# P times V of two pairs in a row, in every second attention step

## The chip, the cores and the metric

The kernel runs on one core of a Trainium2 chip. The metric is the device time of the kernel in microseconds (us), the median of several runs. The engines of the core work side by side and meet through semaphores: TensorE (PE, matmuls; PEld its weight loads), VectorE (DVE), ScalarE (ACT), GpSimd (POOL) and SyncE (SP), which here issues transfers.

## The reference, cut to what matters

The input x is 16 items of 512 tokens x 256. Each item goes through a half feed-forward block, an attention block and another half feed-forward block:

```
x = x + 0.5 * ffn(layernorm(x));  x = x + attn(layernorm(x));  x = x + 0.5 * ffn(layernorm(x))
attn: qkv = x @ w_qkv; 16 heads of 64; sim = (q*SCALE) @ k.T - slope_h*|i-j|, causal
      out = softmax(sim) @ v; return out @ w_out + b_out
ffn:  gelu(x @ w1 + b1) @ w2 + b2      (256 -> 1024 -> 256)
```

## The kernel before, in words

Everything is in float32; a matmul of weights with activations is done as three matmuls (high with high, high with low, low with high). Each engine has its own instruction stream, written out by hand in the order in which it is to run; there is no planner. An engine takes its instructions strictly in that order, and a wait holds all that stands behind it.

The outer loop runs over the items b = 0 to 15. Within an item the heads are taken as eight pairs c = 0 to 7 (two heads a pair). One step c of the attention loop (TensorE: `attention`, L489; ScalarE L650; VectorE L874; GpSimd L1023) has these parts:

- `scores(b, c)` (L432): TensorE computes Q times K transposed of the pair, 8 blocks, in PSUM banks 0 to 5. It waits for the copy of the pair's Q by ScalarE (`proj_copy`), and for VectorE to have read the blocks before.
- `biased` (L833, VectorE): adds the distance bias, finds the row maxima and writes P to SBUF. Blocks go in the order i = 3, 2, 0, 1 (`QORDER`).
- `exps` (L638, ScalarE): exponentials in place, with their sums. `inverse` (L827, VectorE) inverts the sums, `normalise` (L1018, GpSimd) multiplies by them.
- `turned` (L845, VectorE): transposes P in place in 32 x 32 blocks, in two halves. In step c VectorE does `biased(b, c, 3)`, `inverse(b, c-1, 0)`, both halves of `turned(b, c-1)`, and then `biased` of the other blocks. (In step 7 of all items but the last `turned(b, 6, 1)` stands ahead of `biased(b, 7, 3)`.)
- `spread` (L241): 16 transfers bring the blocks of P to the other partitions, into PT (two buffers, by c mod 2). SyncE issues 11 of them, GpSimd 5. They wait for `turned(b, c, 0)` and for P times V of pair c-2, which read the same buffer of PT. P has three buffers.
- `values(b, c)` (L445): TensorE computes P times V of the pair, 12 matmuls in one bank. It waits for the spread of the pair, and for V. `out_copy` (L646, ScalarE) copies its output to SBUF.
- `proj_tile` (L413): K and Q of pair c+1 and one tile of V (none in step 7, two in step 6) by TensorE; ScalarE copies them. They and `values` take turns in banks 6 and 7 (`bank_for`, L341: the bank after `turn[0]` of those in `among[0]`, once what it holds has been read).

Before the change TensorE's step c is scores(c), K and Q of pair c+1, a V tile, values(c-2). In steps 6 and 7 the work of the next item stands between (two layer norm transposes, three of its up projections). ScalarE's step is out_copy(c-3), exps(c,3), copies of K and Q, exps(c,2), copy of V, exps(c,0), exps(c,1).

Of the kernel before, what the change touches and what calls it, by code (L numbers as in the profile page):

```python
def build(nc, x_d, w_qkv_d, w_out_d, b_out_d, w1_d, b1_d, w2_d, b2_d, y_d):
# [11 lines left out]
    NT, NK, NM, NC = T // 128, D // 128, F // 128, H // 2  # L13
# [97 lines left out]
    def v_tiles(c):  # L111
        return {6: [("v", 3, 0), ("v", 3, 1)], 7: []}.get(c, [("v", c // 2, c % 2)] if c >= 2 else [])
# [8 lines left out]
    def steps_v(b, c):  # L121

        if b == 0 and c <= 3:
            return v_tiles(2) + v_tiles(3) if c == 1 else []
        return v_tiles(c)
# [127 lines left out]
    with block:  # L253
# [50 lines left out]
        def _(e):  # L304
            def mm(out, lhsT, rhs, first, last):
                return e.matmul(out, lhsT, rhs, start=first, stop=last)  # L306
# [31 lines left out]
            turn = [7]  # L338
# [93 lines left out]
            def scores(b, c):  # L432
                e.wait_ge(s_pc.sem, s_pc.at((b, ("q", c))))
                for i in QORDER:
                    w = 128 * (i + 1)
                    for h in range(2):
                        if i != 0:
                            bank_free(h + {3: 0, 2: 2, 1: 4}[i])
                            held[h + {3: 0, 2: 2, 1: 4}[i]] = ("scores", b, c, 0 if i == 2 else i, h)
                        hs = slice(64 * h, 64 * h + 64)  # L440
                        keys = qk[c % 2][hs, 1, 0:w].rearrange("p (j m s) -> p m j s", m=4, s=32)
                        mm(score_block(h, i), qk[c % 2][hs, 0, i * 128:i * 128 + 128], keys,
                           True, True).then_inc(s_qk.sem, 1)

            def values(b, c):  # L445
                pv = bank_for(("values", b, c))
                e.wait_ge(s_pc.sem, s_pc.at((b, ("v", c // 2, 1))))
                if b == NB - 1 and c in LAST:
                    e.wait_ge(s_ls[c].sem, s_ls[c].at((b, c)))
                    e.wait_ge(s_la[c].sem, s_la[c].at((b, c)))  # L450
                else:
                    e.wait_ge(s_pt[c % 3].sem, s_pt[c % 3].at((b, c)))
                e.wait_ge(s_pp[c % 3].sem, s_pp[c % 3].at((b, c)))
                for n, (j, blocks) in enumerate(RUNS):
                    i = blocks[0]
                    for h in range(2):
                        p = PT[c % 2][:, 0, block_at(h, i) + 32 * j]
                        step = block_at(h, blocks[-1]) - block_at(h, i)
                        turned = AP(p.tensor, p.offset, [[4 * GW, 128], [step, len(blocks)], [GW, 4], [1, 32]])
                        last = mm(pv[64 * h:64 * h + 64, 128 * i:128 * i + 128 * len(blocks)],  # L460
                                  v[(c // 2) % 2][:, j, 2 * (c % 2) + h, :], turned, n == 0, n == len(RUNS) - 1)
                last.then_inc(s_pv.sem, 1)
# [26 lines left out]
            def attention(b):  # L489
                more = b + 1 < NB  # L490
                begin(b)
                for c in range(2, NC):
                    scores(b, c)
                    if c + 1 < NC:
                        proj_tile(b, ("k", c + 1))
                        proj_tile(b, ("q", c + 1))
                    for tile in steps_v(b, c):
                        proj_tile(b, tile)
                    if more and c == NC - 1:
                        up(1, b + 1, range(2))  # L500
                        among[0] = (0, 1)
                        up(1, b + 1, [2])
                    if more and c == NC - 2:
                        ln_transpose(1, b + 1, 0)
                        among[0] = (5,)
                        ln_transpose(1, b + 1, 1)
                        among[0] = (6, 7)
                    values(b, c - 2)
                    if more and c == NC - 2:
                        turn[0] = 5  # L510
                if more:
                    among[0] = (2, 3, 4, 5)
                    up(1, b + 1, range(3, 6))
                    values(b, NC - 2)
                    among[0] = range(8)
                    up(1, b + 1, range(6, NM))
                    for t in range(3):
                        dn(1, b + 1, t)
                    values(b, NC - 1)
                    dn(1, b + 1, 3)  # L520
                else:
                    among[0] = range(4)
                    for c in range(4):
                        out_part(c, range(NT))
                    among[0] = range(4, 8)
                    values(b, NC - 2)
                    for c in range(4, 6):
                        out_part(c, range(NT))
                    values(b, NC - 1)
                    out_part(6, range(NT))  # L530
                    out_part(7, range(NT))
# [44 lines left out]
        def _(e):  # L576
# [61 lines left out]
            def exps(b, c, i):  # L638
                for h in range(2):
                    e.wait_ge(s_tt.sem, s_tt.at((b, c, i, h)))  # L640
                    p = p_block(c, h, i)
                    r = 2 * (c % 2) + h
                    e.activation(p, p, ACT.Exp, bias=mx[:, r, i:i + 1], scale=-1.0,  # L643
                                 accum_out=sm[:, r, i:i + 1]).then_inc(s_ex.sem, 1)

            def out_copy(b, c):  # L646
                e.wait_ge(s_pv.sem, s_pv.at((b, c)))
                e.activation(o[:, c, :], bank_of(("values", b, c)), ACT.Copy).then_inc(s_oa.sem, 1)

            def attention(b):  # L650
                more = b + 1 < NB
                if b == 0:
                    exps(b, 0, 3)
                    proj_copy(b, tiles[3])
                proj_copy(b, ("k", 1))
                proj_copy(b, ("q", 1))
                for i in QORDER[0 if b > 0 else 1:]:
                    exps(b, 0, i)
                exps(b, 1, 3)
                proj_copy(b, ("k", 2))  # L660
                if b == 0:
                    proj_copy(b, ("q", 2))
                exps(b, 1, 2)
                for tile in steps_v(b, 1)[:1]:
                    proj_copy(b, tile)
                exps(b, 1, 0)
                if b > 0:
                    proj_copy(b, ("q", 2))
                for tile in steps_v(b, 1)[1:]:
                    proj_copy(b, tile)  # L670
                exps(b, 1, 1)
                for c in range(2, NC):
                    if c >= 3:
                        out_copy(b, c - 3)
                    exps(b, c, 3)
                    if c + 1 < NC:
                        proj_copy(b, ("k", c + 1))
                        proj_copy(b, ("q", c + 1))
                    exps(b, c, 2)
                    for tile in steps_v(b, c)[:1]:  # L680
                        proj_copy(b, tile)
                    exps(b, c, 0)
                    for tile in steps_v(b, c)[1:]:
                        proj_copy(b, tile)
                    exps(b, c, 1)
                    if more and c == NC - 2:
                        ln_hi(1, b + 1, 0)
                        ln_hi(1, b + 1, 1)
                if more:
                    gelu(1, b + 1, range(2))  # L690
                    out_copy(b, NC - 3)
                    gelu(1, b + 1, range(2, 6))
                    out_copy(b, NC - 2)
                    gelu(1, b + 1, range(6, NM))
                    out_hi_first(b)
                    out_copy(b, NC - 1)
                else:
                    for c in range(2):
                        out_part_hi(c)
                    spread(e, b, NC - 2, LAST_ACT, s_la[NC - 2])  # L700
                    for c in range(2, 5):
                        out_part_hi(c)
                    out_copy(b, NC - 3)
                    out_part_hi(NC - 3)
                    spread(e, b, NC - 1, LAST_ACT, s_la[NC - 1])
                    for c in (NC - 2, NC - 1):
                        out_copy(b, c)
                        out_part_hi(c)
# [386 lines left out]
```

## Time and profile before

| | before |
|---|---|
| median of 3 runs, us | 2165.0 (2164.84 to 2168.31) |
| span of the profiled execution, us | 2165.1 |
| TensorE busy, us | 2126.9 (98%) |
| VectorE / ScalarE / GpSimd busy, us | 1501.1 / 1238.3 / 1056.3 |
| mean granted TensorE clock | 0.996 |
| transfers of P into PT: by SyncE, by GpSimd | 1398, 640 |

The span runs from the first to the last instruction of one profiled execution; no other time of that execution is given, and the span equals the median of the runs within 0.1 us.
### The profile page before, as it was taken

How to read it: one execution, taken by the hardware profiler on the slowest of the kernel's cores; microseconds unless marked ns; L12 is line 12 of the kernel's file. 1: busy time of each engine (PE TensorE's matmuls, PEld its weight loads, DVE VectorE, ACT ScalarE, POOL GpSimd, SP SyncE). 2: the span in 40 equal slices, each digit the busy share in tenths (PEclk: the TensorE clock that was granted, in tenths of full speed). 3: DMA queues.
4: the chain of work that ended last, by engine and by line, in shares of the span. 5: the costliest groups of instructions: out<-in, count | busy, mean ns of one | idle time of the engine just before them, and what ended most of it. 6: DMA issues, size and time to landing. Idle time of an engine off the chain costs nothing.

```text
span 2165.1 us, 41855 instructions
## 1 busy us (share of the span) xinstructions
PE 2126.9 (98%) x14720; PEld 1739.2 (80%) x14720; DVE 1501.1 (69%) x4031; ACT 1238.3 (57%) x3111; POOL 1056.3 (49%) x1772
## 2 busy tenths in 40 slices
PE   7999999999999999999999999999999999999997
PEld 6688787887878788787887978878787787877866
DVE  6866767667676676776768676676766767667674
ACT  5745646466464664736557365574646646466472
POOL 2744627446273553725537174472744627355371
PEclk9999999999999999999999999999999999999999
DMA  3422505234061441514315052250523405134051
GB/s 132 132 74 75 141 1 158 57 89 127 11 157 50 107 108 31 155 30 118 98 46 145 25 140 76 71 144 3 157 59 93 123 12 155 50 106 110 26 140 51
DMA packets 109985, 193.91 MB, mean 90 GB/s; under 512 B 34512, under 2 KB 53200, under 8 KB 109776
## 3 DMA queue, kind: packets, MB, share of 16 engines
q1 hardware_dynamic: 88816, 137.95, 22.8%
q0 software_dynamic: 20480, 52.47, 9.8%
q8 instruction: 117, 1.92, 0.4%
q10 hardware_dynamic: 480, 0.82, 0.1%
q14 instruction: 92, 0.75, 0.1%
HBM read 14.95 MB, written 8.39 MB: 11 GB/s over the span
## 4 chain that ended last, share of the span: by engine, by line
PE 89%; SPq 4%; DVE 3%; DMA 2%; issue 1%; ACT 1%; POOL 1%; DVEq 0%; POOLq 0%
PE ps L306 87%; SPq L249 3%; PE ps L360 2%; DVE P L848 1%; DMA PT<-P 1%; ACT P L643 1%; DMA out_y<-x 0%; POOL P L1021 0%; POOL PT L249 0%; DVE P L840 0%; DMA raw<-in_L_ffn_w 0%; DVE gl L754 0%; DVE xtl L754 0%; DVE x L787 0%; ACT v L594 0%
## 5 line engine op out<-in xcount | busy, mean ns | idle before, releaser
L1021 POOL TENSOR_SCALAR P<-P,rs 128x512 f32<-128x512 f32 (+3 forms) x1024 | 539.1, 545 | 423.0 <-DVE rs L831 419.7
L643 ACT ACTIVATE P<-P,mx 128x512 f32<-128x512 f32 (+3 forms) x1024 | 562.7, 552 | 186.2 <-DVE mx L840 186.1
L249 POOL DMA_DIRECT2D PT<-P x640 | 322.2, 509 | 249.5 <-DVE P L848 235.6
L848 DVE STREAM_TRANSPOSE P<-P 128x1792 f32<-128x1792 f32 (+1 forms) x256 | 372.3, 1483 | 7.3 <-POOL P L1021 6.8
L306 PE MATMUL ps<-PT,v 128*64 128x256 f32 (+1 forms) x3072 | 305.2, 348 | 8.9 <-DMA PT<-P 8.5
L306 PE MATMUL ps<-qk 64*128 64x512 f32 (+3 forms) x2048 | 311.0, 443 | 0.7 <-ACT qk L594 0.7
L306 PE MATMUL ps<-w2h,gh 128*128 128x256 f32 x1024 | 292.6, 286 | 0.3 <-DVE gl L754 0.3
L306 PE MATMUL ps<-w2l,gh 128*128 128x256 f32 x1024 | 289.7, 283 | 0.0
L306 PE MATMUL ps<-w2h,gl 128*128 128x256 f32 x1024 | 289.6, 283 | 0.0
L306 PEld LDWEIGHTS ps<-PT,v 128*64 128x64 f32 x3072 | 205.5, 137 | 103.8 <-issue 15.1
L594 ACT ACTIVATE qk<-ps 128x512 f32<-128x512 f32 x256 | 153.0, 598 | 230.5 <-PE ps L306 230.5
L840 DVE CUSTOM_DVE_ANT_1 P<-ps,dist 128x384 f32<-128x384 f32 (+2 forms) x768 | 272.3, 414 | 0.0
L612 ACT ACTIVATE gt<-ps,b1c 128x512 f32<-128x512 f32 x256 | 172.9, 688 | 163.3 <-PE ps L306 129.8
L306 PEld LDWEIGHTS ps<-qk 64*128 64x128 f32 x2048 | 166.2, 187 | 114.9 <-issue 73.3
L787 DVE TENSOR_TENSOR x<-ps,x 128x256 f32<-128x256 f32 x192 | 81.0, 422 | 255.5 <-PE ps L306 255.4
L840 DVE CUSTOM_DVE_ANT_0 P<-ps,dist 128x512 f32<-128x512 f32 x256 | 165.7, 684 | 124.9 <-PE ps L306 124.9
L1009 POOL TENSOR_TENSOR rstd<-ve,mhalf 128x4 f32<-128x4 f32 (+1 forms) x50 | 65.2, 1305 | 356.3 <-DVE ve L771 356.3
L306 PE MATMUL ps<-xth,wqh 128*128 128x512 f32 x512 | 210.2, 411 | 1.5 <-DVE xtl L754 1.5
L306 PEld LDWEIGHTS ps<-w2h,gh 128*128 128x128 f32 x1024 | 196.1, 192 | 9.9 <-issue 7.5
L306 PE MATMUL ps<-xtl,wqh 128*128 128x512 f32 x512 | 201.4, 393 | 0.0
L306 PE MATMUL ps<-xth,wql 128*128 128x512 f32 x512 | 200.3, 391 | 0.0
L306 PEld LDWEIGHTS ps<-w2l,gh 128*128 128x128 f32 x1024 | 196.1, 192 | 1.8
(85 smaller groups left out, 4394.7 us busy)
## 6 DMA issues: line engine op xcount, KB each, us to landing
PT<-P SPq DMA_DIRECT2D x1398, 80.0 KB, 2.6
PT<-P POOLq DMA_DIRECT2D x640, 80.0 KB, 2.7
x<-in_L_attn_x SPq DMA_DIRECT2D x16, 512.0 KB, 4.9
out_y<-x SPq DMA_DIRECT2D x15, 512.0 KB, 3.2
raw<-in_L_ffn_w SPq DMA_DIRECT2D x2, 512.0 KB, 5.8
raw<-in_L_ffn_w SPq DMA_DIRECT2D x1, 1024.0 KB, 8.7
rawq<-in_L_attn_w_qkv SPq DMA_DIRECT2D x1, 1024.0 KB, 6.8
rawk<-in_L_attn_w_qkv SPq DMA_DIRECT2D x1, 1024.0 KB, 8.8
```

The source lines that it names most:

```text
L249: e.dma_start(PT[c % 2][32 * m:32 * m + 32, g, :], P[c % 3][32 * g:32 * g + 32, m, :]).then_inc(landed.sem, 16)
L306: return e.matmul(out, lhsT, rhs, start=first, stop=last)
L360: last = e.transpose(dst[:, col:col + 128], xn[:, t, k * 128:(k + 1) * 128], ident[:, :])
L594: e.activation(dst, src, ACT.Copy).then_inc(s_pc.sem, 1)
L612: e.activation(gt[m % 3][:, :], bank_of(("up", f, b, m)), ACT.Gelu, bias=b1c[:, m:m + 1]).then_inc(s_gl.sem, 1)
L643: e.activation(p, p, ACT.Exp, bias=mx[:, r, i:i + 1], scale=-1.0, accum_out=sm[:, r, i:i + 1]).then_inc(s_ex.sem, 1)
L787: e.tensor_tensor(xb[b % 2][:, t, :], bank_of(use)[:, 0:D], xb[b % 2][:, t, :], ALU.add).then_inc(events.sem, 1)
L840: e.tensor_tensor_reduce(out=p_block(c, h, i), in0=score_block(h, i).rearrange("p (m n) -> p m n", m=4), in1=dist[:, :, 128 - 32 * (i + 1) ...
L848: e.transpose(p, p).then_inc(s_tr.sem, 1)
L1009: e.tensor_tensor(rstd[:, L - 1, ts], ve[:, L - 1, ts], mhalf[:, ts], ALU.pow).then_inc(s_pw.sem, 1)
L1021: e.tensor_scalar(p, p, rs[:, 2 * (c % 2) + h, i:i + 1], 1.0, ALU.mult, ALU.mult).then_inc(s_nz.sem, 1)
```

## The change

In the steps c = 3, 5 and 7 TensorE does P times V of pairs c-3 and c-2 directly behind the scores of pair c, ahead of the projections; in the even steps it does none. ScalarE's order follows: in an odd step out_copy(c-3) comes behind exps(c,3) and out_copy(c-2) behind exps(c,2), and the copies of K, Q and V come behind exps(c,0) and exps(c,1). In the even steps its order is as before, without an output copy. The output copy of pair 5 leaves the row of GELUs behind the loop. The banks' turn is set at the start of step 7. VectorE's, GpSimd's and SyncE's streams are not changed.

```diff
--- before.py
+++ after.py
@@ -491,6 +491,11 @@
                 begin(b)
                 for c in range(2, NC):
                     scores(b, c)
+                    if c % 2:
+                        if c == NC - 1:
+                            turn[0] = 5
+                        values(b, c - 3)
+                        values(b, c - 2)
                     if c + 1 < NC:
                         proj_tile(b, ("k", c + 1))
                         proj_tile(b, ("q", c + 1))
@@ -505,9 +510,6 @@
                         among[0] = (5,)
                         ln_transpose(1, b + 1, 1)
                         among[0] = (6, 7)
-                    values(b, c - 2)
-                    if more and c == NC - 2:
-                        turn[0] = 5
                 if more:
                     among[0] = (2, 3, 4, 5)
                     up(1, b + 1, range(3, 6))
@@ -670,26 +672,34 @@
                     proj_copy(b, tile)
                 exps(b, 1, 1)
                 for c in range(2, NC):
-                    if c >= 3:
+                    exps(b, c, 3)
+                    if c % 2:
                         out_copy(b, c - 3)
-                    exps(b, c, 3)
-                    if c + 1 < NC:
+                        exps(b, c, 2)
+                        out_copy(b, c - 2)
+                        exps(b, c, 0)
+                        if c + 1 < NC:
+                            proj_copy(b, ("k", c + 1))
+                        exps(b, c, 1)
+                        if c + 1 < NC:
+                            proj_copy(b, ("q", c + 1))
+                        for tile in steps_v(b, c):
+                            proj_copy(b, tile)
+                    else:
                         proj_copy(b, ("k", c + 1))
                         proj_copy(b, ("q", c + 1))
-                    exps(b, c, 2)
-                    for tile in steps_v(b, c)[:1]:
-                        proj_copy(b, tile)
-                    exps(b, c, 0)
-                    for tile in steps_v(b, c)[1:]:
-                        proj_copy(b, tile)
-                    exps(b, c, 1)
+                        exps(b, c, 2)
+                        for tile in steps_v(b, c)[:1]:
+                            proj_copy(b, tile)
+                        exps(b, c, 0)
+                        for tile in steps_v(b, c)[1:]:
+                            proj_copy(b, tile)
+                        exps(b, c, 1)
                     if more and c == NC - 2:
                         ln_hi(1, b + 1, 0)
                         ln_hi(1, b + 1, 1)
                 if more:
-                    gelu(1, b + 1, range(2))
-                    out_copy(b, NC - 3)
-                    gelu(1, b + 1, range(2, 6))
+                    gelu(1, b + 1, range(6))
                     out_copy(b, NC - 2)
                     gelu(1, b + 1, range(6, NM))
                     out_hi_first(b)
@@ -700,7 +710,6 @@
                     spread(e, b, NC - 2, LAST_ACT, s_la[NC - 2])
                     for c in range(2, 5):
                         out_part_hi(c)
-                    out_copy(b, NC - 3)
                     out_part_hi(NC - 3)
                     spread(e, b, NC - 1, LAST_ACT, s_la[NC - 1])
                     for c in (NC - 2, NC - 1):
```

## Rows read from the trace of the kernel before

**Rows 1.** The profile's page: busy time, share of the span, instructions.

```profile
PE 2126.9 (98%) x14720; PEld 1739.2 (80%) x14720; DVE 1501.1 (69%) x4031; ACT 1238.3 (57%) x3111; POOL 1056.3 (49%) x1772
```

**Rows 2.** TensorE's waits: us in total, times, longest.

```profile
PE ps L306 <- DMA PT<-P: 8.5, 11, 2.0
```

**Rows 3.** Timeline, TensorE, fifth item: start us, us, engine, line, operation, what, count.

```profile
596.93 0.70 PE L306 MATMUL ps<-qk 64*128 64x512 f32 x2
...
603.34 0.28 PE L306 MATMUL ps<-wql,xth 128*128 128x256 f32 x1
603.46 0.28 PE L306 MATMUL ps<-wqh,xtl 128*128 128x256 f32 x1
603.67 2.38 PE L306 MATMUL ps<-PT,v 128*64 128x256 f32 x24
605.98 0.70 PE L306 MATMUL ps<-qk 64*128 64x512 f32 x2
...
608.34 0.50 PE L306 MATMUL ps<-xth,wqh 128*128 128x512 f32 x1
608.68 0.40 PE L306 MATMUL ps<-xtl,wqh 128*128 128x512 f32 x1
...
612.72 0.44 PE L306 MATMUL ps<-PT,v 128*64 128x256 f32 x2
...
615.03 0.70 PE L306 MATMUL ps<-qk 64*128 64x512 f32 x2
```

**Rows 4.** Timeline, VectorE, the same step (2.61 is idle time before).

```profile
607.14 0.69 DVE L840 CUSTOM_DVE_ANT_0 P<-ps,dist 128x512 f32<-128x512 f32 x1 [2.61 <-PE ps L306]
...
608.46 2.87 DVE L848 STREAM_TRANSPOSE P<-P 128x1792 f32<-128x1792 f32 x2
```

**Rows 5.** Timeline, SyncE's queue, last issues of pairs 1 and 3.

```profile
610.07 0.59 SPq L249 DMA_DIRECT2D PT<-P  x1
...
628.09 0.59 SPq L249 DMA_DIRECT2D PT<-P  x1
```

**Rows 6.** Chain that ended last, fourth item, around pair 2's P times V.

```profile
487.32 2.05 DMA PT<-P
...
489.62 9.12 PE ps L306 x64
```

**Rows 7.** Timeline, TensorE and SyncE, second and sixth item: scores, last issue.

```profile
199.36 0.70 PE L306 MATMUL ps<-qk 64*128 64x512 f32 x2
...
211.65 0.59 SPq L249 DMA_DIRECT2D PT<-P  x1
...
747.71 0.70 PE L306 MATMUL ps<-qk 64*128 64x512 f32 x2
...
759.67 0.69 SPq L249 DMA_DIRECT2D PT<-P  x1
```

**Rows 8.** Timeline, TensorE and SyncE, fifth item, steps 6 and 7.

```profile
633.12 0.70 PE L306 MATMUL ps<-qk 64*128 64x512 f32 x2
...
644.49 0.70 PE L306 MATMUL ps<-qk 64*128 64x512 f32 x2
...
646.15 0.59 SPq L249 DMA_DIRECT2D PT<-P  x1
...
657.83 0.44 PE L306 MATMUL ps<-PT,v 128*64 128x256 f32 x2
```

**Rows 9.** Timeline, ScalarE, fifth item, copy of Q in step 3.

```profile
611.39 0.60 ACT L594 ACTIVATE qk<-ps 128x512 f32<-128x512 f32 x1 [0.76 <-PE ps L306]
```

**Rows 10.** Timeline, TensorE, after idle time (in brackets, with its releaser).

```profile
73.88 1.48 PE L306 MATMUL ps<-PT,v 128*64 128x256 f32 x11 [2.05 <-DMA PT<-P]
...
2114.45 0.53 PE L306 MATMUL ps<-woh,fh 128*128 128x256 f32 x1 [2.49 <-DVE fl L754]
...
2117.77 0.36 PE L306 MATMUL ps<-woh,fh 128*128 128x256 f32 x1
```

**Rows 11.** Stretch: us, busy us of five engines, PEclk, DMA share, GB/s.

```profile
2116.00:2118.00 2.00, 2.00 (x12) 2.00 (x11) 0.20 (x1) 0.00 (x0) 0.90 (x2) 0.51 0.84 264
```

## The prediction

> **What bounds the kernel now.** I read the busy table, then TensorE's own waits, then the timeline of one item (the fifth, b = 4) engine by engine. In the busy table TensorE is at 98% [rows 1], and the table of its waits holds only 8.5 us of waiting for the spread transfers, in 11 places, none over 2.0 us [rows 2]. So it is a kernel in which time is TensorE's stream of work, and the question for any change of order is whether that stream still finds its data ready. One step of the steady part is 9.05 us: scores at 605.98, K, Q and V projections from 608.34, P times V at 612.72, next scores at 615.03 [rows 3].
>
> I write S(c) for the start of a step's scores, PV(c) for the start of P times V of pair c. From the rows: scores take 2.36 us (605.98 to 608.34), PV 2.31 (603.67 to 605.98), the three projections 4.38 (608.34 to 612.72) [rows 3].
>
> What PV(c-2) waits for is a long chain that starts at S(c-1). VectorE writes the first biased block 1.16 us after those scores (607.14), then inverts, and turns pair c-2 in place, ending at 608.46 + 2.87 = 611.33, S + 5.35 [rows 4]. Only then can SyncE issue its 11 spread transfers, one behind the other: for pair 1 the last issue is at 610.07 [rows 5], which is S(2) + 13.14 [rows 3]. Where TensorE did wait, the last issue at 487.32 landed after 2.05 us and PV began at 489.62 [rows 6]: a PV can start 2.30 us after the last issue. In the fifth item pair 1 is therefore ready at 610.07 + 2.30 = 612.37, and TensorE came to it at 612.72 [rows 3]. The slack is 0.35 us. This is what the 98% hides: the PV stands about as early as its data allow.
>
> **The change, part by part.**
>
> *TensorE, odd steps.* PV(c-2) is moved ahead of K, Q and V, and PV(c-3) from the end of the even step before to a place just behind S(c). The even step becomes scores and three projections: 2.36 + 4.38 = 6.74 us. This uses that scores enter behind a projection as PV does; PV entered 0.21 us behind the last V matmul (603.46 to 603.67) [rows 3], which I take for both. In the odd step TensorE wants PV(c-3) at S(c) + 2.36 and PV(c-2) at S(c) + 4.67, that is at S(c-1) + 6.74 + 4.67 = S(c-1) + 11.41. Before, the same PV(1) came at S(2) + 15.79. It is asked for 4.4 us earlier, and the chain that makes its data is not touched: S(c-1), VectorE's order, and SyncE's 11 issues stay.
>
> *The first such place, c = 3.* Ready at S(2) + 13.14 + 2.30 = +15.44, wanted at +11.41: a stall of 4.03 us. TensorE then has 2.31 of PV and 4.38 of projections to S(4), at S(2) + 22.13, against 615.03 - 596.93 = 18.10 before: 4.03 us lost. In the second item, where the last issue is earliest, it is S(2) + 12.29 (199.36 to 211.65) [rows 7], a loss of 3.2; worked as here, the mean over the 16 items is 3.9 us.
>
> *The second, c = 5.* Pair 3's last issue is at 628.09, S(4) + 13.06 [rows 3, 5]; in the sixth item it is only S(4) + 11.96 (747.71 to 759.67) [rows 7], since one slow issue is missing. Losses 3.97 and 2.8; the mean over the items is 3.4.
>
> *The third, c = 7.* Step 6 is longer (a second V tile, eight transposes). From S(6) at 633.12 to PV(6) at 657.83 it was 24.71 us [rows 8]. Step 6 alone was 11.36 (to S(7) at 644.49). The order now is step 6 without PV (11.36 - 2.31 = 9.05), scores, PV(4), PV(5), six up tiles, PV(6). PV(5) is wanted at S(6) + 13.72 and is ready at 646.15 + 2.30 = +15.33 [rows 8]: 1.6 us of stall, of which about 1.4 is lost up to PV(6); where pair 5's issues end a microsecond earlier I put the loss at 0.4. I take 0.8 between them. In the last item PV(5) waited already, and I count nothing.
>
> *Even steps, PV(c-3), and the batch's other PVs.* PV(c-3) was ready a step earlier: nothing. PT has two buffers, so the spread of pair c-1 now waits for PV(c-3) in odd steps, on SyncE and on GpSimd's queue. That PV ends at S(c) + 4.67, the turn at S(c) + 5.35: nothing, and the work queued behind that wait is not held. In a stalled step SyncE itself is issuing pair c-2 until about S(c) + 7, so pair c-1 starts 1.5 us late; it is wanted a whole pair of steps later, so this costs nothing.
>
> *ScalarE.* out_copy(c-2) now stands amid the exponentials, waits for PV(c-2), and behind it are exps(c,0), the K copy, exps(c,1) and the Q copy, on which S(c+1) waits. With P = PV(c-2): copy of the output P + 2.4 to 3.0, exps 0.8, K copy (ready at about P + 4.0) to P + 4.6, exps 1.0, Q copy to P + 6.2. TensorE wants S(c+1) at P + 6.69. Covered, by 0.5 us only. In the even step the order is as before and the Q copy ends at S + 6.01 (611.99) [rows 9], TensorE wants the next scores at S + 6.74: covered by 0.7 us.
>
> *Switches of tile shape.* Scores, PV and projections use the array in three shapes. The first projection matmul behind scores takes 0.34 us to the next where 0.23 is usual (608.34 to 608.68) [rows 3]; with about 0.1 ahead of it, a switch is some 0.2 us. Two steps had six of them and now have five, since PV follows PV; the new one, scores to PV, no row shows: its bounds are 0 and 0.4, and I take the nearest rows' 0.2. So 48 places gain 0.1 us on average between the bounds: 5 us. The Trainium skill (TensorEngine Tiling (Array Packing), Key Properties) says that a change of tiling mode drains TensorE; the rows agree with 0.2 us. By that rule alone, with all data in time, the change would give 48 x 0.2 = 10 us, which is the rival on the other side.
>
> *TensorE's clock.* After an idle 2.05 us (at 73.88) the granted clock stayed at 2.4 GHz; after an idle 2.49 us (at 2114.45) [rows 10] it was at 1.2 GHz (0.51 in the stretch 2116 to 2118) [rows 11] and the 256-column matmuls came every 0.221 us from 2114.45 to 2117.77 (15 intervals), where they come every 0.12 at the full clock (603.34 to 603.46) [rows 3, 10]. Such a stretch costs 15 x 0.10 = 1.5 us. My stalls at c = 3 and 5 are 2.9 to 4.4 us, 32 of them, all longer than 2.49. Bounds are 0 and 32 x 1.5 x 2 = 96 us (two stretches each). One row at 2.49 us doesn't say that every idle of that kind does it, so I let three in four do it: 36 us. The Trainium skill (TensorE: Matmul & The Clock Gate, HAM oscillation) tells of this pattern: a wait for data that comes back in each round throws the engine back to the low clock each time. By that rule it would be all 32, 48 us and 2338 us in total; without it the sum ends at 2290.
>
> **Sum.** 16 x (3.9 + 3.4 + 0.8) = 130; less 5; plus 36: 161 us. The profiled span is 2165.1 us, the median of the three runs 2165.0, so nothing of size lies around the span. 2165 + 161 = 2326 us.
>
> **Rivals.**
> 1. *Stalls, but the clock holds.* 2165 + 130 - 5 = 2290 us. For it: one fall at one idle of 2.49 us is thin, and PV and scores may keep the clock up. Against: the stalls here are longer. 0.23.
> 2. *ScalarE becomes the gate.* The 0.5 us of cover goes if the output copy or the exponentials come 1.5 us later than worked out; S(c+1) is then 1 us late in each odd step: 48 us more, 2372. 0.07.
> 3. *The other side: the data are in time.* It takes the last issue to be by S(c-1) + 11.41 - 2.30 = 9.11, nearly 3 us sooner than the earliest shown, 11.96 [rows 7]; only if VectorE turned pair c-2 before it needs S(c-1) could that be, and its first biased block stands ahead in its order [rows 4]. Then TensorE gains the switches alone, 48 x 0.2 = 10 us: 2155. 0.05.
> 4. *Half of it.* The spread of odd pairs is quicker in the new rhythm (fewer slow issues, 1 us less in each), or the loss is given back at an item's end: stalls of 2 us at c = 3 and 5, none at 7, no clock falls: about 2225 us. 0.08.
>
> **How the numbers follow.** My forecast has 0.57. Its own range is 2295 to 2360: stall means 0.5 us either way (16 each) and the clock at 15 to 50 us. Rival 1 is inside the range if it reaches down to 2265; rival 2 ends at about its top. 2265 to 2370 leaves out rivals 3 and 4 and half of 2, under 2 in 10. A measurement of this kernel can tell about 0.2% (4 us) from no change: faster 0.05 (rival 3), the same 0.02, slower 0.93.
>
> **What would show it.** Right: TensorE's waits for the spread transfers grow from 8.5 us to about 150, in about 45 places, at PV(1), PV(3), PV(5), with last issue to PV at 2.30 us; no wait at PV(0), (2), (4); busy share down to some 92%; S(2) to S(4) 22 us with the clock full, more with it low; the granted clock's mean near 0.98; no wait of TensorE for ScalarE at scores. Wrong: PV(c-2) starting 11.4 us behind S(c-1) without a wait; the waits in full but the clock at 1.00 (rival 1); S(c+1) released by a Q copy (rival 2).

## The result, and the profile after

| | before | after |
|---|---|---|
| median of 4 runs, us | 2164.92 (2164.64 to 2168.31) | 2336.22 (2327.07 to 2337.73) |
| ratio, 95% interval | | 1.0779 (1.0759 to 1.0800) |
| span of the profiled execution, us | 2165.1 | 2333.3 |
| mean granted TensorE clock | 0.996 | 0.974 |

The change costs 7.8%: 2336 us where 2326 was predicted, in a range of 2265 to 2370. The page's busy table has the same number of instructions on every engine, and nearly the same busy time on all but TensorE:

```profile
PE 2178.3 (93%) x14720; PEld 1777.4 (76%) x14720; DVE 1500.7 (64%) x4031; ACT 1244.4 (53%) x3111; POOL 1051.2 (45%) x1772
```

The profiled execution itself was timed at 2335.1 us, 1.8 us more than its span, and so it is in the other runs. TensorE's share fell from 98% [rows 1] to 93%, though its busy time grew by 51 us: the same 14720 matmuls, part of them at the low clock. Its waits (us in total, times, longest), which stood at 8.5 us in 11 places [rows 2]:

```profile
PE ps L306 <- DMA PT<-P: 119.5, 41, 5.1
...
PE ps L306 <- DVE xtl L763: 7.5, 17, 1.5
...
PE ps L306 <- ACT qk L596: 2.1, 3, 0.8
```

The wait for the spread transfers is now the one of size, and no wait for ScalarE is. The timeline of TensorE in the fifth item, steps 2 to 7 (the answer to [rows 3, 8]; in brackets the idle time and its releaser):

```profile
638.36 2.43 PE L306 MATMUL ps<-qk 64*128 64x512 f32 x16
...
645.10 2.43 PE L306 MATMUL ps<-qk 64*128 64x512 f32 x16
647.46 2.38 PE L306 MATMUL ps<-PT,v 128*64 128x256 f32 x24
653.48 4.53 PE L306 MATMUL ps<-PT,v 128*64 128x256 f32 x24 [3.64 <-DMA PT<-P]
...
662.70 2.43 PE L306 MATMUL ps<-qk 64*128 64x512 f32 x16
669.44 2.43 PE L306 MATMUL ps<-qk 64*128 64x512 f32 x16
671.79 2.38 PE L306 MATMUL ps<-PT,v 128*64 128x256 f32 x24
677.86 2.38 PE L306 MATMUL ps<-PT,v 128*64 128x256 f32 x24 [3.68 <-DMA PT<-P]
684.57 2.43 PE L306 MATMUL ps<-qk 64*128 64x512 f32 x16
693.63 2.42 PE L306 MATMUL ps<-qk 64*128 64x512 f32 x14
696.35 0.70 PE L306 MATMUL ps<-qk 64*128 64x256 f32 x2 [0.30 <-DVE xtl L763]
696.98 2.38 PE L306 MATMUL ps<-PT,v 128*64 128x256 f32 x24
699.72 2.38 PE L306 MATMUL ps<-PT,v 128*64 128x256 f32 x24 [0.36 <-DMA PT<-P]
```

Read it from start to start. The even step is 6.74 us (638.36 to 645.10), PV(0) starts 2.36 us behind the scores without a wait, and PV(1), asked for at S(2) + 11.41, starts at S(2) + 15.12: a stall of 3.71 us. It then takes 4.53 us where PV(0) took 2.38. From PV(1) to S(4) it is 9.22 us; from PV(3) to S(6) it is 6.71, which is the sum of a PV and three projections at the full clock.

The chain that ended last, in the same place (start us, us, what), shows what PV(1) stood behind:

```profile
641.04 2.80 DVE P L857 x2
...
650.41 0.59 SPq L249
...
651.04 2.19 DMA PT<-P
653.24 0.25 issue
653.48 10.39 PE ps L306 x52
```

The turn of pair 1 ends at 643.84, then come SyncE's 11 issues, then the landing of the last: the chain of [rows 5, 6] in the same order, with the engine now waiting at its end. From the start of the last issue to PV(1) it is 2.44 us here, where 2.30 was reckoned. For the granted clock, stretches of four us from the start of three PVs on (us, busy us of five engines, PEclk, DMA share, GB/s): PV(1) and PV(3) of the fifth item, and PV(3) of the third, with that PV's own row behind them:

```profile
653.48:657.48 4.00, 4.00 (x22) 2.70 (x24) 1.04 (x9) 0.70 (x4) 3.96 (x9) 0.50 0.78 208
```
```profile
391.57:395.57 4.00, 4.00 (x25) 3.01 (x26) 3.60 (x17) 1.66 (x5) 3.26 (x6) 0.62 0.52 141
...
677.86:681.86 4.00, 4.00 (x31) 3.22 (x32) 3.02 (x11) 1.98 (x8) 3.97 (x7) 1.00 0.77 211
```
```profile
391.57 3.61 PE L306 MATMUL ps<-PT,v 128*64 128x256 f32 x24 [2.69 <-DMA PT<-P]
```

0.50 is 1.2 GHz, 1.00 is 2.4 GHz. PV(1) of the fifth item ran at the low clock, PV(3) of the same item at the full one, behind a wait that was as long. In PV(3) of the third item the clock fell on the way: 0.62 is the mean of four us that began at the full clock and ended at the low one.

Where the 168 us are (16 items, each stretch from start to start, after less before): S(2) to S(4) **+90.4**, S(4) to S(6) **+62.6**, S(6) to PV(6) **+14.9**, all the rest +0.3. Of these, what PV(1) to S(4) and PV(3) to S(6) take beyond 6.69 us, the length at the full clock, goes with the low clock: 29.3 us in all 16 items at c = 3, 12.5 us in 7 of the 16 at c = 5. **Together: 42 us of clock, 126 us of waiting** (the little that the new order gives back is already taken off, see Switches below).

### The profile page after: what moved, and what is told of

The parts are those of the page before. It is cut to its first block, busy times and chain, and to the rows that moved or that the text cites. A ratio compares the mean times of both kernels' runs of the same rounds, so it can differ in the third digit from the quotient of the medians.

```text
span 2333.3 us, 41855 instructions
## 1 busy us (share of the span) xinstructions
PE 2178.3 (93%) x14720; PEld 1777.4 (76%) x14720; DVE 1500.7 (64%) x4031; ACT 1244.4 (53%) x3111; POOL 1051.2 (45%) x1772
## 4 chain that ended last, share of the span: by engine, by line
PE 68%; SPq 14%; DVE 7%; DMA 5%; issue 3%; ACT 2%; POOL 0%; ACTq 0%; DVEq 0%
PE ps L306 66%; SPq L249 14%; DVE P L857 4%; DMA PT<-P 4%; PE ps L360 1%; DMA out_y<-x 1%; ACT P L645 1%; DVE P L849 1%; DVE xtl L763 1%; ACT v L596 0%; DVE x L796 0%; ACT qk L596 0%; DMA raw<-in_L_ffn_w 0%; POOL P L1030 0%; ACT xth L606 0%
## 5 line engine op out<-in xcount | busy, mean ns | idle before, releaser
L1030 POOL TENSOR_SCALAR P<-P,rs 128x512 f32<-128x512 f32 (+3 forms) x1024 | 532.0, 537 | 569.7 <-DVE rs L840 566.3
L306 PE MATMUL ps<-PT,v 128*64 128x256 f32 (+1 forms) x3072 | 341.2, 377 | 119.7 <-DMA PT<-P 119.5
L306 PEld LDWEIGHTS ps<-PT,v 128*64 128x64 f32 x3072 | 232.8, 149 | 230.2 <-issue 162.4
L857 DVE STREAM_TRANSPOSE P<-P 128x1792 f32<-128x1792 f32 (+1 forms) x256 | 372.6, 1484 | 28.6 <-POOL P L1030 28.1
L306 PE MATMUL ps<-qk 64*128 64x512 f32 (+3 forms) x2048 | 321.8, 444 | 8.0 <-DVE xtl L763 4.5
L306 PEld LDWEIGHTS ps<-w2h,gh 128*128 128x128 f32 x1024 | 196.1, 191 | 10.2 <-issue 7.5
```

The costliest lines, as they stand in the source:

```text
L857: e.transpose(p, p).then_inc(s_tr.sem, 1)
L1030: e.tensor_scalar(p, p, rs[:, 2 * (c % 2) + h, i:i + 1], 1.0, ALU.mult, ALU.mult).then_inc(s_nz.sem, 1)
```

## The experiments

All times are medians in us; ratios stand against the kernel before, run on the same chip (2165.93, 2165.37 and 2165.34 us in the three groups of runs). The change itself was not run again beside the experiments; the kernel before, which was, moved by less than 1.1 us from group to group. The table gives the three stretches in us, summed over the 16 items, after subtracting those of before, and TensorE's waits for the spread in us.

| kernel | median | ratio (95%) | S(2)-S(4) | S(4)-S(6) | S(6)-PV(6) | waits for spread |
|---|---|---|---|---|---|---|
| the change | 2336.22 | 1.0779 (1.0759 to 1.0800) | 90.4 | 62.6 | 14.9 | 119.5 |
| 1 exponentials first | 2343.34 | 1.0826 (1.0805 to 1.0848) | 84.3 | 59.7 | 28.6 | 120.1 |
| 2 second PV late | 2271.18 | 1.0491 (1.0472 to 1.0511) | 52.6 | 37.4 | 14.8 | 1.7 |
| 3 fill | 2296.85 | 1.0610 (1.0594 to 1.0625) | 65.4 | 51.7 | 11.8 | 9.8 |
| 4 eight and eight | 2305.06 | 1.0640 (1.0618 to 1.0661) | 61.6 | 41.9 | 24.8 | 72.4 |
| 5 second PV late, old copy order | 2184.24 | 1.0086 (1.0073 to 1.0100) | -0.2 | 0.6 | 15.7 | 4.9 |
| 6 both at the end | 2197.57 | 1.0149 (1.0135 to 1.0163) | 10.9 | 10.2 | 8.3 | 3.3 |
| 7 K and Q between | 2269.29 | 1.0481 (1.0467 to 1.0496) | 47.3 | 35.4 | 17.5 | 7.8 |
| 8 second PV early, alone | 2329.28 | 1.0757 (1.0743 to 1.0772) | 96.7 | 54.9 | 9.4 | 131.9 |
| 9 first PV later, alone | 2165.73 | 1.0003 (0.9994 to 1.0012) | -0.1 | 0.6 | -1.3 | 6.2 |
| 10 K and Q between, copies first | 2213.52 | 1.0226 (1.0212 to 1.0240) | 19.0 | 9.7 | 17.7 | 26.5 |
| 11 both at the end, V copy first | 2193.83 | 1.0132 (1.0118 to 1.0146) | -0.9 | 18.0 | 10.2 | 6.0 |

### Which half of the move costs: 8 and 9

Experiment 8 (of the change): PV(c-2) alone stands behind the scores, PV(c-3) goes back to the even step.

```diff
-                        values(b, c - 3)
                         values(b, c - 2)
...
+                    if c % 2 == 0:
+                        values(b, c - 2)
```

> Only pair c-2 is moved ahead of the projections; pair c-3 stays at the end of the even step as in the kernel before. Pair c-2 is then asked for at the same 11.41 us behind the scores of the step before. Theory A: the same stalls as in the changed kernel, and the clock falls: 2335 us, range 2310 to 2355. Rival C (the delay of pair c-3 makes a good part of the loss): below 2280.

Experiment 9 (of the kernel before): PV(c-3) alone behind the scores.

```diff
                     scores(b, c)
+                    if c in (3, 5):
+                        values(b, c - 3)
...
-                    values(b, c - 2)
+                    if c in (3, 5, 6, 7):
+                        values(b, c - 2)
```

> The kernel before, with only the other half of the move: in steps 3 and 5 P times V of pair c-3 stands directly behind the scores (it comes out of the even step before), P times V of pair c-2 stays at the end of the odd step, steps 6 and 7 are as before. ScalarE's output copy of pair c-3 stands behind exps(c,3) in steps 3 and 5. Theory A (the whole loss is pair c-2 asked for 4.4 us too soon, and taking pair c-3 later is free, as the prediction says): 2165, within 4 us; no wait of TensorE for the spread above the 8.5 us of before; the steps 2 to 4 and 4 to 6 take together what they took. Rival C (the second limit, the spread of pair c-1 that waits for P times V of c-3 and the late turn in the odd step, costs TensorE something by itself): a wait at P times V of the even pair or at scores, 0.5 us or more in each of 32 places, 2180 or more. Rival D (the new switch scores to P times V is dear by itself, 0.3 us or more over a switch between other shapes): 32 x 0.3 = 10 us more, 2175, in which scores to P times V shows over 2.6 us from start to start.

Measured: 2329.28 and 2165.73 us. The one half has nearly all of the loss (164 of 171 us), the other, in steps 3 and 5, none (1.0003). Step 7 is as before in experiment 9; what PV(c-3) costs there is in experiment 5. TensorE in the fifth item, first of experiment 8, then of experiment 9:

```profile
638.02 2.43 PE L306 MATMUL ps<-qk 64*128 64x512 f32 x16
...
653.64 4.53 PE L306 MATMUL ps<-PT,v 128*64 128x256 f32 x24 [4.14 <-DMA PT<-P]
```
```profile
597.91 2.43 PE L306 MATMUL ps<-qk 64*128 64x512 f32 x16
604.65 2.43 PE L306 MATMUL ps<-qk 64*128 64x512 f32 x16
607.01 2.38 PE L306 MATMUL ps<-PT,v 128*64 128x256 f32 x24
613.70 2.38 PE L306 MATMUL ps<-PT,v 128*64 128x256 f32 x24
616.01 2.43 PE L306 MATMUL ps<-qk 64*128 64x512 f32 x16
```

In 8 the data come at S(2) + 15.62 and the wait is there; in 9 S(2) to S(4) is 18.10 us, as before the change [rows 3], and PV(1) at S(2) + 15.79 finds its data. VectorE's turn is as late in experiment 9 as in the change (it ends at S(3) + 7.26), without harm. The entry of PV behind scores is 2.36 us from start to start, as that of the projections was [rows 3]: the new switch has the old price.

### The dose: 10, and what it took to see it

Experiment 7 (of the change): K and Q stand between the two PVs, so that PV(c-2) is asked for 2.9 us later.

```diff
                         values(b, c - 3)
-                        values(b, c - 2)
...
                         proj_tile(b, ("q", c + 1))
+                    if c % 2:
+                        values(b, c - 2)
```

> The changed kernel, with the projections of K and Q between pair c-3 and pair c-2, a smaller dose of the same thing. Theory A: pair c-2 is asked for 14.17 us behind the scores of the step before in place of 11.41, so that the stalls are 1.2, 0.7 and (step 7, not touched) 0.8 us, too short for the clock to fall; two switches more: 2165 + 16 x 2.7 + 5 = 2213 us, range 2195 to 2235. If the cost is two pairs in a row or the place of pair c-3 and not how early pair c-2 is asked for, it stays above 2280 or falls to 2165.

Experiment 2 (of the change): PV(c-2) back at the end of the odd step, that is where it was.

```diff
-                        values(b, c - 2)
...
+                    if c % 2:
+                        values(b, c - 2)
```

> The changed kernel, but pair c-2 goes back to the end of the odd step (pair c-3 stays directly behind the scores). Theory A: P times V of pair c-2 is wanted 15.8 us behind the scores of the step before, as in the kernel before, so the whole loss goes: 2165 us within 5, waits for the transfers under 15 us, granted clock 0.99 or more. If the delay of pair c-3 by a step is what costs (rival C: it holds back the buffer PT and so the spreads), the time stays above 2250.

Both missed, 2269.29 and 2271.18 us, with hardly a wait for the spread left. The timelines of VectorE, ScalarE and TensorE of experiment 2 in step 3 of the fifth item (S(3) = 631.64) show what had taken its place:

```profile
636.02 2.90 DVE L861 STREAM_TRANSPOSE P<-P 128x1792 f32<-128x1792 f32 x2 [1.41 <-POOL P L1034]
...
639.42 0.61 ACT L646 ACTIVATE P<-P,mx 128x384 f32<-128x384 f32 x1 [2.38 <-DVE mx L853]
...
640.63 1.06 ACT L597 ACTIVATE qk<-ps 128x512 f32<-128x512 f32 x2
...
641.26 0.39 PE L306 MATMUL ps<-wqh,xth 128*128 128x256 f32 x1 [1.93 <-ACT qk L597]
```

VectorE's turn ends at S(3) + 7.28, not at + 5.35 as it did before [rows 4]; exps(c,2) needs the block behind the turn; and in both kernels I had put the K and Q copies behind exps(c,2), so TensorE waited for their banks (65.6 us in 34 places in experiment 2, with a granted clock of 0.986 in the mean beside it). My own edit of ScalarE's order was the fault, not TensorE's order. So both were run again with the copies ahead of exps(c,2): experiment 5 from 2, experiment 10 from 7.

```diff
-                        exps(b, c, 2)
                         if c + 1 < NC:
                             proj_copy(b, ("k", c + 1))
                             proj_copy(b, ("q", c + 1))
+                        exps(b, c, 2)
```

> As the run with the second pair back at the end of the odd step (2271 us), but with ScalarE's copies of K and Q ahead of exps(c,2), as in the kernel before. In that run TensorE waited 65.6 us for copies of K and Q and no longer for the transfers; exps(c,2) hung on VectorE's turn, which is late in odd steps, and the copies stood behind it. Theory A with this correction: no wait is left, 2165 us within 6. Rival C (it is the delay of pair c-3, through the buffer PT and GpSimd's row, that costs 105 us): it stays above 2240.

> A dose between the change and the kernel before: P times V of pair c-3 behind the scores, then K and Q of pair c+1, then P times V of pair c-2, then the V tile; ScalarE copies K and Q ahead of exps(c,2), so that no copy stands behind VectorE's late turn. Theory A (time is lost only by how much sooner P times V of pair c-2 is asked for than its data land): TensorE comes to it 3.0 us later than in the change, so the stalls shrink from about 4.0 and 3.4 to 1.0 and 0.5 us, and the clock falls in few places or none: 2165 + 16 x 1.5 + about 16 us at the item's end and for single places where the clock falls = 2205, range 2190 to 2235. Rival E (the loss does not follow the distance, for instance because the order of the shapes on TensorE or the output copy's place costs it): within 10 us of the 2269 that the same order of TensorE gave with the copies behind the late turn.

Measured 2184.24 and 2213.52 us: the second inside its range, the first 13 us above the "2165 within 6". Now the loss in S(2) to S(6) follows the distance. PV(c-2) asked for at S(c-1) + 15.8 (experiment 5, as before): 0.4 us lost in S(2) to S(6) over all items. At + 14.36 (experiment 10; K and Q stand ahead, 2.9 us): 28.7 us, 0.9 per stall. At + 11.41 (the change): 153.0 us. Data that come at about + 15.1 (638.36 to 653.48) give 0.7 us for experiment 10 (0.9 measured in the mean; over the items PV starts between + 14.36 and + 17.55) and 3.7 for the change; what the change loses beyond that is the clock, which held in experiment 10 (mean 0.996).

Experiment 5 still loses 18.9 us against the kernel before (17.3 in the profiled executions). Of this 15.7 is in S(6) to PV(6), and a row of the change shows where it comes from: with PV(4) gone from step 6, scores(7) stand directly behind the layer norm's transposes, and their last block needs bank 5, which VectorE has yet to read. TensorE and VectorE of the change:

```profile
692.66 1.03 PE L360 MATMUL ps<-ident,xn 128*128 128x128 f32 x8
```
```profile
695.01 1.29 DVE L763 TENSOR_TENSOR xtl<-ps,xth 128x512 fp32r<-128x512 f32 x2 [0.30 <-ACT xth L606]
```

S(7) to PV(4) is 3.35 us there (693.63 to 696.98) and 3.35 in experiment 5; without that wait it is 2.36. That is 0.99 us in each of the 15 items with a next one, 14.9 us in all. Experiment 9, which leaves step 6 alone, doesn't have it. So taking PV(c-3) later is free at c = 3 and 5, and costs a microsecond at c = 7.

### The clock: 3

Experiment 3 (of the change): 13 projection matmuls more ahead of PV(1) and PV(3), into PV's bank, whose result the PV overwrites. They lie in the wait; at c = 5 they outlast it by a little in 11 of the 16 items, where PV(3) starts at S(4) + 14.58 without idle time.

```diff
+                for _ in range(fill):
+                    mm(pv, wqh[:, 0, 0:128], xth[:, 0, :], True, True)
...
-                        values(b, c - 2)
+                        values(b, c - 2, 13 if c < NC - 1 else 0)
```

> The changed kernel with 13 projection matmuls of 512 columns more (3.0 us; their result is overwritten) in the wait between the two pairs, in steps 3 and 5. It separates the clock from the wait. Theory A with the clock: the fill lies inside waits of 2.9 to 4.4 us, keeps TensorE busy, and the granted clock stays at 1.0 there: S(2) to S(4) falls from about 23.5 to 22.1 us, and the total from 2336 to 2300 within 10. Rival D (what looks like a loss by the clock is part of the wait): no gain, 2336 or up to 20 more, since two switches of shape are added.

Measured 2296.85 us: TensorE does more work and the kernel is 39 us faster. The same four us behind PV(1) of the fifth item:

```profile
643.47:647.47 4.00, 4.00 (x31) 3.22 (x32) 0.79 (x6) 1.81 (x7) 3.97 (x8) 1.00 0.79 220
```

31 matmuls in four us at 1.00, against 22 at 0.50 in the change. PV(1) to S(4) is 6.69 (643.47 to 650.16), and the clock is at 1.00 in the four us behind each of the 32 PVs. The waits themselves stay: S(2) to S(6) still loses 117.1 us, where the change without its clock lost 111.2. So the two parts separate as the timeline had them: all 42 us of clock came back, the waits took 6 more, and 39 us is what was left of it in the median, with some 4 us less in the other stretches.

### The length of the data's chain: 4

Experiment 4 (of the change): SyncE issues 8 of the 16 transfers, GpSimd 8.

```diff
-    SPREAD_SP, SPREAD_POOL = GROUPS[:11], GROUPS[11:]
+    SPREAD_SP, SPREAD_POOL = GROUPS[:8], GROUPS[8:]
```

> The changed kernel with the 16 spread transfers of a pair issued 8 by SyncE and 8 by GpSimd in place of 11 and 5. Theory A (SyncE's row of issues is the last part of the chain): the last issue comes 3 x 0.64 = 1.9 us sooner, the stalls fall to about 2.0, 1.5 and 0 us at c = 3, 5, 7, too short for the clock to fall often: 2165 + 16 x 3.5 - 5 = 2216 us, range 2195 to 2245. Rival E (the transfers' own bandwidth sets when they land, not their issue): landing moves by less than 0.5 us and the time stays above 2300.

Measured 2305.06 us, well short of the expected 2216, and in the "above 2300" of rival E, though not for its reason: the landing did move, by more than a microsecond. The chain of waits in the fifth item:

```profile
632.81 2.80 DVE P L857 x2
...
640.37 0.60 SPq L249
...
641.01 2.90 DMA PT<-P
643.91 0.25 issue
644.16 5.92 PE ps L306 x40
```

From the end of the turn (635.61) to PV(1) it is 8.55 us, against 9.64 in the change (643.84 to 653.48). Three issues fewer save 1.8 (5.3 us from the first issue to the end of the last, against 7.1); 0.7 of it goes back in the landing (2.90 us against 2.19, from the start of the last issue). The medians from issue to landing say the same (GpSimd's queue had 2.7 in the change); experiment 4, then the change:

```profile
PT<-P POOLq DMA_DIRECT2D x1024, 80.0 KB, 2.9
PT<-P SPq DMA_DIRECT2D x1020, 80.0 KB, 3.1
```
```profile
PT<-P SPq DMA_DIRECT2D x1398, 80.0 KB, 2.6
```

So the same transfers, issued closer together and half of them by the other queue, landed later; which of the two did it was not tried. Over all 32 places the stalls shrank by 38.6 us, 1.2 each, where 1.9 was expected; with fewer low clocks (mean 0.984) S(2) to S(6) gained 49.5 us. The rest of the shortfall is in three other things. The clock, which was to fall seldom, still fell in 12 of 16 items at c = 3 (in none at c = 5). TensorE now waits for output copies, 9.9 us in 30 places, behind PV(3) among others. And 9.9 us went back in S(6) to PV(6), about as much again outside the three stretches.

### ScalarE's order: 1

Experiment 1 (of the change): all exponentials of the odd step ahead of out_copy(c-2) and the copies.

```diff
-                        exps(b, c, 2)
+                        for i in QORDER[1:]:
+                            exps(b, c, i)
                         out_copy(b, c - 2)
-                        exps(b, c, 0)
...
-                        exps(b, c, 1)
```

> The changed kernel, but in odd steps ScalarE does all the exponentials ahead of the output copy of pair c-2 and the copies of K, Q and V. Theory A (the stall is TensorE's wait for the spread transfers of pair c-2, ScalarE's order is covered): as the changed kernel, 2336 us within 6, waits of TensorE for the transfers about 120 us. Rival B (the output copy amid the exponentials holds ScalarE, VectorE and GpSimd back and so makes the spreads late): the exponentials of pair c come up to 5 us sooner, and the time falls by 20 us or more, below 2316.

Measured 2343.34 us, 7 us slower and not 20 faster, and the waits for the transfers are the same (120.1 us): that the exponentials wait behind the output copy is not the cause. What is left over comes from two shifts that pull against each other: the clock fell in fewer places (mean 0.980), and S(6) to PV(6) lost 13.7 us more, with a new wait of TensorE for output copies (12.3 us in 13 places).

### Two in a row without asking early: 6 and 11

Experiment 6 (of the kernel before): in steps 3 and 5 PV(c-3), then PV(c-2), both at the end.

```diff
-                    values(b, c - 2)
+                    if c in (3, 5):
+                        values(b, c - 3)
+                    if c in (3, 5, 6, 7):
+                        values(b, c - 2)
```

> The kernel before, with pair c-3 moved from the end of the even step to the end of the odd step 3 and 5, just ahead of pair c-2: two pairs in a row, but behind the projections, with ScalarE's order as before and both output copies at the start of the even step. Theory A: pair c-2 is asked for as late as before (15.7 us behind the scores of the step before), so there is no wait, and one switch of shape of six is gone in 32 places: 2165 - 6 = 2159 us, within 4. Rival C (pair c-3 later by a step holds the spread of pair c-1 on SyncE and GpSimd, and so the normalisation behind it): slower than 2175.

Experiment 11 is 6 with ScalarE's V copy ahead of exps(c,2) in those steps.

```diff
+                    if early:
+                        for tile in steps_v(b, c):
+                            proj_copy(b, tile)
                     exps(b, c, 2)
```

> Two P times V in a row at the end of steps 3 and 5 (pair c-3, then pair c-2), steps 6 and 7 as before, and ScalarE's V copy of those steps ahead of exps(c,2). Before it stood behind exps(c,2), and the second P times V waited for the V copy's bank: 2198 in that form, with 0.7, 0.6 and 0.5 us lost per item in the three stretches. Theory (the bank waits are all that was lost there): the first two losses go to about 0.2 each, 2165 + 16 x 0.2 x 2 + 8 = 2179, range 2165 to 2190; TensorE's waits for copies of V fall from 35 us to below 10. If two P times V in a row save a switch that is worth 0.1 us or more, it comes out at 2165 or below. Rival F (the K bank is held by the first P times V's output until its output copy, which waits for nothing but stands behind the exponentials of the next step): the losses stay at 0.5 us or more per item and stretch, 2190 or more.

Measured 2197.57 and 2193.83 us: both orders lose, the theory's 2159 and 2179 missed, and both times fall where the rivals C and F had put them. TensorE's waits in experiment 6, then 11:

```profile
PE ps L306 <- ACT v L597: 12.5, 31, 2.9
PE ps L306 <- ACT qk L597: 9.4, 17, 0.7
```
```profile
PE ps L306 <- ACT qk L597: 17.5, 17, 1.4
```

With the V copy moved, the first stretch lost nothing (-0.9 us) and the second lost more, to copies of K or Q that come late. GpSimd in both waits about 100 us for PV (107.2 and 100.2) ahead of its spread issues, since PV(c-3) now ends only with the odd step; that this delays normalising, turn, exponentials and so the copy is how I read it, and was not tried. That PV(c-2) is not asked for early keeps the waits for the spread down, at 3.3 and 6.0 us. One more thing these runs show, where nothing waits. TensorE in the fifth item of experiment 11:

```profile
604.96 2.43 PE L306 MATMUL ps<-qk 64*128 64x512 f32 x16
...
618.44 4.55 PE L306 MATMUL ps<-PT,v 128*64 128x256 f32 x48
622.91 2.43 PE L306 MATMUL ps<-qk 64*128 64x512 f32 x16
```

Two PVs in a row take 4.47 us where two single ones take 2 x 2.31, and S(2) to S(4) is 17.95 us against 18.10: a switch of shape saved is worth 0.15 us. The Trainium skill (TensorEngine Tiling (Array Packing), Key Properties) says that a change of tiling mode drains TensorE; the row agrees, and gives the price here. None of the orders tried here beats the kernel before.

## Why the prediction was right, point by point

- *What bounds it, and the first stall.* Right. Predicted for the fifth item: ready at S(2) + 15.44, a stall of 4.03; measured + 15.12, a stall of 3.71. Without the clock S(2) to S(4) lost 61.1 us, 3.8 per item, where 3.9 was predicted. That it fits so closely is in part luck: the last issue came 0.3 us sooner than before in the mean of the first 15 items, and from its start to PV(1) it was 2.57 us, not 2.30, since it does not always land as fast as in [rows 6]. For the same reason the slack before was not 0.35 us: in the fifth item the trace of before has the transfers of pair 1 landed at 612.40, and with 0.25 us from landing to PV that leaves 0.07. Pair 3 had more, about 0.9 in the mean. Experiments 5, 8, 9 and 10 show that the distance by which PV(c-2) is asked too soon is the cause of the loss at c = 3 and 5.
- *The second stall.* Predicted 3.4 per item, measured (62.6 - 12.5) / 16 = 3.1; here the 2.30 us held, and the last issue came 0.35 sooner than before.
- *The third.* The size was right (0.8 predicted, 0.9 measured), the reason only half, so the size is luck. I had the layer norm's transposes in the step's length and did not ask who reads their bank next: scores(7) wait 1.0 us for VectorE, and PV(5) then waits only 0.4 more for its spread, not 1.6. The data come at S(6) + 15.15 (684.57 to 699.72; predicted + 15.33), so in this item the first wait hides in the second. Over the items the wait at scores(7) is 14.9 us, PV(5)'s own is 5.6 in eight of the first 15 items, where about 13 was predicted, and 5 to 6 come back by the shorter order (see Switches). In experiment 5, where no spread is late but the last item's, the first stands alone.
- *Waits in the profile.* Some 150 us in 45 places was too much, 119.5 in 41 is what the terms above leave: the stalls of the 32 places, start to start, are 115 us.
- *Clock.* Predicted: in three of four of 32 stalls, 1.5 us each, 36 us. Measured: in 23 of 32, 1.8 us each, 42 us. Of the 23 falls 17 show 0.57 to 0.67 over the four us from PV's start and cost 1.6 us in the mean, as priced from [rows 10]. The other six were longer, 0.50 all through these four us, as in the row of 653.48, and cost 2.5 us; [rows 10] had no such fall. By the rule of the Trainium skill that I cited (TensorE: Matmul & The Clock Gate, HAM oscillation) it would be all 32; the trace agrees at c = 3 (16 of 16) and not at c = 5 (7 of 16).
- *Switches.* The size came out, the places did not. I took 5 us off, in 48 places. A switch saved ahead of PV(1) or PV(3) saves nothing while that PV waits for data, so 32 of the 48 gave nothing. At c = 7 the new order has two switches fewer, and an item in which PV(5) doesn't wait shows what it gave: in the second item S(6) to PV(6) is 25.38 us, 24.39 without the 0.99 at scores(7), against 24.71 before. That is 0.3 to 0.4 us an item, 5 to 6 in all; that it is the switches is by its size (0.15 us each by experiment 11), not by a run of its own.
- *"The turn at S(c) + 5.35" in the odd step: nothing.* The number failed: as in experiment 2, in the change it ends at S(3) + 7.28. GpSimd's five issues for pair 1 come 2.3 us nearer to the scores, since the even step is shorter, and normalising stands behind them:

```profile
644.42 2.51 POOL L249 DMA_DIRECT2D PT<-P  x5 [1.65 <-DVE P L857]
646.96 4.09 POOL L1030 TENSOR_SCALAR P<-P,rs 128x512 f32<-128x512 f32 x8
```
```profile
649.48 2.90 DVE L857 STREAM_TRANSPOSE P<-P 128x1792 f32<-128x1792 f32 x2 [1.41 <-POOL P L1030]
```

  The "nothing" held all the same: experiment 9 shows the late turn harmless with the old order of the copies. In the change the stall for PV(c-2) is longer than this delay, which is how I read it there. With the copies behind exps(c,2) it cost 87 us (experiment 2 against 5) and 56 us (7 against 10).
- *ScalarE covered by half a microsecond.* Right, and as thin: the Q copy ends at 662.07 for S(4) at 662.70, and 0.64 us ahead of S(6) in the same item, where the clock was full.

```profile
661.49 0.58 ACT L596 ACTIVATE qk<-ps 128x512 f32<-128x512 f32 x1
```

- *Sum.* 130 of waiting less 5 for the switches was predicted, 126 measured with the switches in it; 36 of clock, 42 measured. That is 1 and 6 us more: 2333, the span of the profiled execution. The median of the runs lies 3 us above it; 1.8 of them are time outside the span, which the prediction took for nothing.

## What to carry to other kernels

A busy share of 98% says nothing of how early each piece of work stands: before an instruction is moved ahead, take the slack of its data from the rows (here the landing of the last transfer against PV's start, under 0.4 us for pair 1), for here all that was beyond the slack came back as a wait, one for one. A wait of some microseconds on TensorE in each round cost more than itself here (42 us on top of the 115); matmuls without use, laid into it, gave 39 us back. And when an experiment moves work back and the time doesn't return, look in the waits for what your own edit has moved beside it, before you doubt the theory.

## What was not expected of the hardware

- Waits of the same length end with either clock: behind 3.68 us idle PV(3) of the fifth item ran at 2.4 GHz, behind 2.69 us in that of the third item the clock fell to 1.2 (0.62 over its four us). At c = 3 the clock fell in all 16 items, at c = 5 in 7. The 2.49 us of idle time in [rows 10], by which the prediction called its stalls long enough, are no lower bound either. TensorE in the 13th item of experiment 4, with the stretch from the same start:

```profile
1771.70 3.78 PE L306 MATMUL ps<-PT,v 128*64 128x256 f32 x24 [1.99 <-DMA PT<-P]
```
```profile
1771.70:1775.70 4.00, 4.00 (x25) 2.96 (x26) 4.00 (x15) 1.49 (x5) 0.68 (x2) 0.60 0.13 32
```

  In the third item of the same run a wait of 2.97 us was followed by 1.00, and so was the one of 2.05 us in [rows 10]. What tells them apart stays open.
- Issuing 16 transfers of 80 KB by two queues of 8, rather than 11 and 5, moved the median from issue to landing from 2.6 to 3.1 us on SyncE's queue and gave back 0.7 of the 1.8 us that the quicker issuing had won in the fifth item (0.7 of 2.0 in the mean of the items at c = 3).
